# Windowed attention with keys at their position modulo 128, a V tile mixed by DMA, and proportions scaled by GpSimd

## The reference, cut to what matters

```python
def local_attention(q, k, v):                 # WINDOW = 64, QK_SCALE = 8
    bq = q.reshape(b, h, w, WINDOW, d) * QK_SCALE
    bk, bv = (look_around(bk), look_around(bv))   # the window before and this one
    sim = jnp.einsum('bhwid,bhwjd->bhwij', bq, bk)
    mask = (i < j) | (i > j + WINDOW) | (j == -1)
    attn = jax.nn.softmax(jnp.where(mask, -max, sim), axis=-1)
    out = jnp.einsum('bhwij,bhwjd->bhwid', attn, bv)

def _layer(x, ...):                           # 8 heads of 64 features
    q, k, v = split(shift_token(x) @ wqkv, 3)
    q, k = rotary_xpos(l2norm(q) * qs, l2norm(k) * ksc)
    x = x + local_attention(q, k, v) @ wo
    h = layernorm(shift_token(x)) * lg + lb
    a, g = split(h @ w1 + b1, 2)
    return x + (a * gelu(g)) @ w2 + b2
```

## Time and profile before

| what | value |
|---|---|
| median of 3 runs | 3171.33 us (3165.91 to 3173.92) |
| the profiled execution's own time | 3165.32 us |
| its span, first to last instruction | 3163.5 us |
| busy share of PE, DVE, ACT, POOL | 79%, 78%, 63%, 38% |
| first and last `reciprocals` of the first stack | 407.9 and 1354.0 us |
| the same of the second stack | 2176.7 and 3131.7 us |

### The profile page before, as it was taken

The page is one execution under the profiler, slowest core; times in us unless marked ns, Lnnn a source line. Parts: engine busy times, 40 slices in busy tenths (PEclk is TensorE's granted clock), DMA queues, the critical chain, the costliest instruction groups (busy, mean ns, idle before and its releaser), DMA issues. The chain is left out here.

```text
span 3163.5 us, 44621 instructions
## 1 busy us (share of the span) xinstructions
PE 2507.0 (79%) x12492; PEld 1338.3 (42%) x12492; DVE 2454.7 (78%) x5574; ACT 1977.9 (63%) x4833; POOL 1207.6 (38%) x1052
## 2 busy tenths in 40 slices
PE   7999688888888888866767667667888888888887
PEld 3555345445444444422222222223444545444444
DVE  2333388888888888848988989987888888888886
ACT  3444266666656665658777776765666666665664
POOL 1222232233332322228777777763333232223220
PEclk9999799999999999978888898898999999999999
DMA  2000000000000000000000000000000000000000
GB/s 116 1 0 0 1 1 1 1 1 1 1 1 1 1 0 0 1 0 1 1 1 1 0 1 0 0 1 1 1 1 1 0 1 1 1 8 4 4 4 11
DMA packets 1942, 13.50 MB, mean 4 GB/s; under 512 B 192, under 2 KB 192, under 8 KB 1216
## 3 DMA queue, kind: packets, MB, share of 16 engines
q1 hardware_dynamic: 1728, 11.24, 0.9%
HBM read 9.14 MB, written 2.10 MB: 4 GB/s over the span
## 5 line engine op out<-in xcount | busy, mean ns | idle before, releaser
L488 POOL TENSOR_TENSOR arena<-arena 128x512 f32<-128x512 f32 x256 | 325.1, 1270 | 1179.9 <-DVE arena L1439 1179.9
L1368 DVE RECIPROCAL RC<-LS 128x256 f32<-128x256 f32 x256 | 446.9, 1746 | 1.7 <-ACT P L1048 1.5
L514 POOL TENSOR_TENSOR arena<-arena 128x512 f32<-128x512 f32 x256 | 329.0, 1302 | 121.1 <-ACT arena L1208 117.8
L1076 ACT ACTIVATE arena<-psum 128x512 f32<-128x512 f32 x256 | 152.7, 596 | 313.0 <-PE psum L789 312.7
L492 POOL TENSOR_TENSOR arena<-arena,SC 128x512 f32<-128x512 f32 x256 | 267.3, 1044 | 197.6 <-DVE SC L1450 196.9
L1054 ACT ACTIVATE arena<-psum 128x512 f32<-128x512 f32 x256 | 152.6, 596 | 282.4 <-PE psum L699 270.2
L789 PE MATMUL psum<-rest,HA 128*128 128x512 f32 x512 | 277.3, 624 | 55.0 <-DVE arena L1439 55.0
L1525 DVE TENSOR_TENSOR_SCAN arena<-arena,psum 128x512 f32<-128x512 f32 x256 | 310.9, 1214 | 3.2
L740 PE MATMUL psum<-HN,rest 128*128 128x512 f32 (+1 forms) x384 | 217.8, 676 | 113.2 <-ACT arena L1091 79.5
L875 PE MATMUL psum<-BS,tabs 96*128 96x512 bf16 x384 | 143.4, 434 | 202.8 <-DVE arena L1525 201.2
L944 PE MATMUL psum<-arena,first 128*128 128x512 f32 x512 | 284.5, 644 | 11.6 <-POOL arena L505 11.2
(11 more groups left out here) (220 smaller groups left out, 6024.5 us busy)
## 6 DMA issues: line engine op xcount, KB each, us to landing
rest<-in_rest SPq DMA_DIRECT2D x1, 4183.0 KB, 22.5
X<-in_x SPq DMA_DIRECT2D x1, 2048.0 KB, 10.5
out<-X SPq DMA_DIRECT2D x8, 256.0 KB, 2.0
first<-in_first SPq DMA_DIRECT2D x1, 1445.5 KB, 6.1
tabs<-in_tabs SPq DMA_DIRECT2D x1, 1248.0 KB, 13.1
```

The source lines that it names most:

```text
L488: nc.gpsimd.tensor_tensor(CQ[:, part, :], CQ[:, part, :], SQN[:, part, :], ALU.add).then_inc(f_rope, 1)
L514: nc.gpsimd.tensor_tensor(WU[:, k % DEEP, :], RG[:, k % DEEP, :], U[t.j % 2][:, k % 2, :], ALU.mult).then_inc(m_wu, 1)
L1368: v.reciprocal(RC[:, 2 * (g % 2):2 * (g % 2) + 2, :].rearrange("p t (r d) -> p t r d", r=2), LS[:, g % 2, :, :].unsqueeze(3).to_broadcast( ...
```

## The change

1. Scores: every head has 2 x 128 columns of keys instead of 128 + 192. For the second 128 queries the key of position p stands in column p modulo 128: columns 128 to 191 of the bank hold keys 128 to 191 for all of these queries; columns 192 to 255 hold keys 64 to 127 for queries 128 to 191 and keys 192 to 255 for queries 192 to 255 (two products of 64 x 64 on halves of the output partitions). `band` follows this.
2. `maxima` and `exponentials`: four pieces of 128 x 128 per unit.
3. V: a mixed tile, whose lower 64 rows are keys 192 to 255 and whose upper 64 rows are keys 64 to 127, as `mixed_values` in the diff has it, is made per sequence by two DMAs of 64 x 512 fp32 from SBUF to SBUF, issued by SP. The output DMAs now stand in the same queue behind them, slot by slot.
4. `reciprocals` is 128 x 4 (`RS`). GpSimd multiplies the 128 x 512 proportions in `P` in place (`proportions`), between its two older operations.
5. `flip`: four transposes into one bank; the two banks alternate with the unit. ACT alone copies it (`flipped`), 128 x 512. `flipped_dve` is gone.
6. `weigh`: per head one product of 128 columns and two of 64. `output` is a plain copy. The wait for the output of the unit before moves from the copies to `weigh`.
7. Orders: on DVE `sums` and `products` come before `output`, and `reciprocals` before the third quarter step. On ACT both exponentials come first, `features` before `norms`, and the first two copies of V at the start of steps 1 and 2.

```diff
...
-BF, N_BF = layout([("ident16", 128), ("band", 384), ("causal", 384), ("sel", 32 * 128)])
+BF, N_BF = layout([("ident16", 128), ("band", 256), ("causal", 384), ("sel", 32 * 128)])
...
-        ARENA = 25088
+        ARENA = 27136
...
-        VT = [shared("layers", [128, 4, INNER]) for _ in range(2)]
+        VT = [shared("layers", [128, 6, INNER]) for _ in range(2)]
...
-        RC = sb("RC", [128, 4, 128])
-        P = sb("P", [128, 4, 384])
+        RS = sb("RS", [128, 2, 2, 2])
+        P = sb("P", [128, 4, 256])
...
-        f_rc = sem("f_rc")
+        f_rs = sem("f_rs")
+        f_rp = sem("f_rp")
-        f_ptd = sem("f_ptd")
...
+        f_vm = (sem("f_vm0"), sem("f_vm1"))
...
-    with sp_.Fori(0, PAIRS) as i:
-        sp_.wait_ge(f_x, i + (PAIRS + 1))
-        sp_.dma_start(out[:, bass.ds(i * NT, NT)], X[:, bass.ds(i * NT, NT)]).then_inc(out_done, 16)
+    def mixed_values(k, b):
+        v = VT[k.side(1)]
+        k.wait_ge(f_v, 4, 2 * b + 2, slot=1)
+        sp_.dma_start(v[0:64, 4 + b, :], v[0:64, 2 * b + 1, :]).then_inc(f_vm[b], 16)
+        sp_.dma_start(v[64:128, 4 + b, :], v[64:128, 2 * b, :]).then_inc(f_vm[b], 16)
+    def sp_slot(k):
+        if k.pre:
+            mixed_values(k, 0)
+            mixed_values(k, 1)
+        if k.ph and k.post and k.layer(-1) == DEPTH - 1:
+            k.wait_pair(f_x, -1)
+            sp_.dma_start(out[:, k.tokens(-1)], X[:, k.tokens(-1)]).then_inc(out_done, 16)
+    for ph in range(2):
+        passes(sp_, ph, sp_slot)
...
+    def rotated(k, m, n):
+        k.wait_ge(f_prod, 8, n + 1, slot=m)
+        nc.gpsimd.tensor_tensor(CQ[:, n % 2, :], CQ[:, n % 2, :], SQN[:, n % 2, :], ALU.add).then_inc(f_rope, 1)
+    def scaled(k, m, n):
+        k.wait_ge(f_rope, 8, n + 1, slot=m)
+        k.wait_ge(f_sc, 8, n + 1, slot=m)
+        heads = CQ[:, n % 2, :].rearrange("p (h d) -> p h d", d=DH)
+        nc.gpsimd.tensor_tensor(heads, heads, SC[:, n % 2, :].unsqueeze(2).to_broadcast([128, HEADS, DH]),
+                                ALU.mult).then_inc(f_qk, 1)
+    def proportions(k, m, g):
+        s = g % 2
+        k.wait_ge(f_rs, 8, g + 1, slot=m)
+        p = P[:, 2 * s:2 * s + 2, :].rearrange("p r (t c) -> p (r t) c", t=2)
+        nc.gpsimd.tensor_tensor(p, p, RS[:, s, :, :].rearrange("p r t -> p (r t)").unsqueeze(2).to_broadcast([128, 4, 128]),
+                                ALU.mult).then_inc(f_rp, 1)
     def pool_slot(k):
...
+        for g in range(8):
+            if item(k, 4 * g, 2):
+                rotated(k, *item(k, 4 * g, 2))
+            if k.heads(g + 1):
+                proportions(k, *k.heads(g + 1))
+            if item(k, 4 * g, 2):
+                scaled(k, *item(k, 4 * g, 2))
...
+        at = SEQ * b
...
+            mm(s[:, 0:128], q[rows, at:at + 128], key[rows, at:at + 128], start=True, stop=True)
...
+            mm(s[:, 128:192], q[rows, at + 128:at + 256], key[rows, at + 128:at + 192], start=True, stop=True)
+        for s, rows in halves:
+            mm(s[0:64, 192:256], q[rows, at + 128:at + 192], key[rows, at + 64:at + 128], start=True, stop=True)
+        for s, rows in halves:
+            mm(s[64:128, 192:256], q[rows, at + 192:at + 256], key[rows, at + 192:at + 256],
     def flip(k, m, g):
...
+        k.wait_ge(f_rp, 8, g + 1, slot=m)
+        k.wait_ge(f_pta, 8, g - 1, slot=m)
...
+            for tile in range(2):
+                at = 256 * r + 128 * tile
+                last = nc.tensor.transpose(P_BANK[g % 2][:, at:at + 128],
+                                           P[:, 2 * (g % 2) + r, 128 * tile:128 * tile + 128], F("ident"))
+        last.then_inc(f_ptp, 1)
     def weigh(k, m, g):
+        k.wait_ge(f_oe, 8, g, slot=m)
...
+            k.wait_ge(f_vm[b], 32, 32, slot=m)
+        v = VT[k.side(m)]
+        halves = [(O_BANK[64 * r:64 * r + 64, :], slice(DH * (2 * j + r), DH * (2 * j + r) + DH),
+                   PT[:, g % 2, 256 * r:256 * r + 256]) for r in range(2)]
+        for o, head, pt in halves:
+            mm(o[:, 0:128], v[:, 2 * b, head], pt[:, 0:128], start=True, stop=True)
+        for o, head, pt in halves:
+            mm(o[:, 128:192], v[:, 4 + b, head], pt[:, 128:192], start=True, stop=True)
+        for o, head, pt in halves:
+            last = mm(o[:, 192:256], v[:, 2 * b + 1, head], pt[:, 192:256], start=True, stop=True)
...
     def exponentials(k, m, g, r):
...
+        A(p[:, 0:128], p[:, 0:128], ACT.Exp, bias=NB[:, s, r, 0:1], scale=-1.0, accum_out=LS[:, s, r, 0:1])
+        A(p[:, 128:256], p[:, 128:256], ACT.Exp, bias=NB[:, s, r, 1:2], scale=-1.0,
+          accum_out=LS[:, s, r, 1:2]).then_inc(f_exp, 1)
+    def flipped(k, m, g):
+        k.wait_ge(f_pv, 8, g - 1, slot=m)
+        k.wait_ge(f_ptp, 8, g + 1, slot=m)
+        A(PT[:, g % 2, :], P_BANK[g % 2], ACT.Copy).then_inc(f_pta, 1)
...
+        if item(k, h, 7):
+            features(k, *item(k, h, 7))
...
+        if k.pre and h in (14, 30):
+            values(k, (14, 30).index(h) + 2)
     def act_slot(k):
         for g in range(8):
+            if k.pre and g in (1, 2):
+                values(k, g - 1)
             if k.heads(g + 1):
                 exponentials(k, *k.heads(g + 1), 0)
+                exponentials(k, *k.heads(g + 1), 1)
             if k.heads(g):
-                flipped_act(k, *k.heads(g))
-            act_dense(k, 4 * g)
-            if k.heads(g + 1):
-                exponentials(k, *k.heads(g + 1), 1)
-            for h in range(4 * g + 1, 4 * g + 4):
+                flipped(k, *k.heads(g))
+            for h in range(4 * g, 4 * g + 4):
                 act_dense(k, h)
...
     def maxima(k, m, g, r):
...
+        v.tensor_tensor_reduce(p[:, 0:128], S_BANK[r][:, 0:128], T16("band", 0, 128), -1.0, 3e38,
+                               ALU.add, ALU.min, NB[:, s, r, 0:1])
+        v.tensor_tensor_reduce(p[:, 128:256], S_BANK[r][:, 128:256], T16("band", 128, 256), -1.0, 3e38,
+                               ALU.add, ALU.min, NB[:, s, r, 1:2]).then_inc(f_nb, 1)
     def reciprocals(k, m, g):
...
+        v.reciprocal(RS[:, g % 2, :, :], LS[:, g % 2, :, :]).then_inc(f_rs, 1)
+    def before_maxima(k, g):
+        if k.heads(g):
+            k.wait_ge(f_ptp, 8, k.heads(g)[1] + 1, slot=k.heads(g)[0])
...
+            k.wait_ge(f_sim, 16, 2 * k.heads(g + 2)[1] + 2, slot=k.heads(g + 2)[0])
     def output(k, m, g):
...
+        k.wait_ge(f_pv, 8, g + 1, slot=m)
+        before_maxima(k, 8 * m + g + 1)
+        v.tensor_copy(OT[k.side(m)][:, j, SEQ * b:SEQ * b + SEQ], O_BANK[:, 0:256]).then_inc(f_oe, 1)
...
     def dve_slot(k):
         for g in range(8):
+            dve_dense(k, 4 * g)
             if k.heads(g - 1):
                 output(k, *k.heads(g - 1))
-            dve_dense(k, 4 * g)
-            if k.heads(g):
-                flipped_dve(k, *k.heads(g))
+            else:
+                before_maxima(k, g)
             if k.heads(g + 2):
                 maxima(k, *k.heads(g + 2), 0)
             dve_dense(k, 4 * g + 1)
             if k.heads(g + 2):
                 maxima(k, *k.heads(g + 2), 1)
-            dve_dense(k, 4 * g + 2)
             if k.heads(g + 1):
                 reciprocals(k, *k.heads(g + 1))
+            dve_dense(k, 4 * g + 2)
             dve_dense(k, 4 * g + 3)
...
+    k1 = np.where((q < 64) & (k >= 64), k, k + 128)
...
+    band = np.concatenate([ok0, ok1], 1)
```

61 lines of the change are left out of this document (removed).

## The result

The changed kernel takes 2901.68 us (median of 4 runs, 2894.18 to 2904.42), beside 3169.84 us of the kernel before on the same chip: ratio 0.915, 95% interval 0.9129 to 0.9172, 268 us less. The forecast was 2936 us, 235 less. The time is right within 35 us; of the reasons, half fell in the experiments, so part of the agreement is luck; the part on the prediction tells where.

The account below looks back on a forecast made before the run. DVE and PE, waiting for each other, were taken as the bound. Slots falling from 61.7 to 54.5 us gave 201 us over 28 slots, edges 34; 3165.3 less 235 is 2930, plus 6 is 2936 us, range 2860 to 3065.

Parts of the forecast that it names:

- What bounds the kernel: Both stacks: DVE and PE mostly run side by side but each waits for the other; 61.7 us per slot.
- Rival 1: PE, ACT and `T_BANK` hold steps 1 to 5; only steps 0, 6 and 7 shrink: 3059 us, chance 0.15.
- PE's block: `weigh`, `scores` and `flip` on PE: 2.01 us, at most 2.56, taken as 2.15, a gain of 0.34.
- the straight line: PE's score products: cost extrapolated from 192 and 128 columns, four of 64 at 0.21 us; block 2.01 us.
- rival 4: PE's small products cost their upper bound, 0.4 us more per step where PE ends last: 2996 us, within the forecast's 0.69.
- steps 4 and 5: Gelus keep 5.66 us, exponentials to `features` shrinks from 2.65 to 2.0, shorter block before: 16.5 us instead of 17.66.
- Steps 1 to 3: Three blocks give 1.0 us, 0.7 us DVE waits go in two steps, step 3 stays ACT's: 20.5 instead of 23.65.
- Step 0: `HA` written ahead of `sums` makes the `QK_BANK` cycle about 1 us longer: 5.4 us instead of 7.4.
- Step 6: Only PE's block shortens it: 6.2 us instead of 6.45.
- step 7: `to_features`, its copy, a V projection and `project` in a row: 5.4 us instead of 6.5.
- the cover: PE's other work between two flips just covers the 3.25 us from one flip through `output`, `reciprocals` and `proportions` to the next.
- Rival 3: DVE and GpSimd exclude each other, a slot needing 64.5 us: slower, 3250 us, chance 0.04.

Follow-up runs that it names:

- b1: The kernel before with only the reciprocal taken of 128 x 4 and a DVE copy spreading it to 128 x 256: 3166.98 us, ratio 0.9977.

## Why the prediction was right in the time and half wrong in the reasons

- **What bounds the kernel.** This step failed. The prediction took the 180.1 us before `output` for half of an exchange ("has PE waiting for DVE's copies on its other side"), and let DVE's relief shorten the steps. b1 shows that alone it does not, and PE's waits of the kernel before, shown there, could have told it: 1.7 us for DVE's flip copy and 11.2 for the reciprocals. Idle time before `output` shows that DVE waited for PE; that PE waited for DVE in turn was assumed. Rival 1 had the right premise (PE, ACT and `T_BANK` hold the steps) and the wrong time, since the change moved ACT's order as well.
- **DVE.** The groups' busy times drop by 607.6 us, as forecast (446.9 + 174.4 + 105.2 + 179.3 + 146.2 less 147.0 + 145.6 + 107.2 + 44.6). The engine's total is at 1983, not 1850: 85 us are on L1480, L1431, L1388 and L1389, some 15 are other small growth and 36 that groups overlap less.
- **PE's block.** 1.96 us, just under the straight line (2.01) and below the 2.15 taken; the bound of 2.56 for products of 64 x 64, and with it rival 4, is out. `scores` takes 0.87 us (607.51 to 608.38) for 0.95. 0.53 us less per unit at the rate of the doubled flip (63 us per 0.47) is 71 us, an estimate.
- **ACT.** The prediction gave its orders a place in steps 4 and 5 alone (16.5 us forecast, 16.50 measured) and none elsewhere. They are the largest part of the account below: 96 us for `exponentials` and `features`, 58 for the V copies. Of the 96, 15 are the clock of step 5, which the prediction did not have at all.
- **The sum from the runs.** 96 + 58 + 71 + 13 (the small reciprocal beside ACT's order, from two runs whose intervals overlap) = 238 of 268 us. This is an account and not a proof: 96 and 13 were measured in the kernel before, 58 and the rate of the 71 in the changed one. The remaining 30 can be DVE's order, its flip copy and the parts' influence on each other; no run assigns them. The parts aren't independent: ACT's order alone rids the kernel before of all its long steps 5, and the changed kernel has 9 of them again; and undone one at a time, five of them cost 165 + 134 + 63 + 58 + 37 = 457 us, the 37 with the tiny copies in it.
- **The steps.** Steps 1 to 3 were forecast at 20.5 and came to 18.76, since the V copies weren't seen. Step 0 was forecast at 5.4 and came to 6.66 from 7.05; `HA` before `sums` holds it more than the 1 us that was put down: its two writes take 831 + 587 ns and DVE idles 1.3 us before them (42.4 over 32). Step 6 5.93 for 6.2, step 7 5.34 for 5.4. Step 7's number was right with the wrong cause: the block gives 0.5 of its 1.5 us, ACT's order the rest. Steps 4 and 5 came out at 16.50 for 16.5, but with 0.5 us of clock in them that the forecast had not counted: the slot that it read (17.66 us) was a short one, the mean of the kernel before is 18.24. So the time of 2936 us owes something to luck: step 0 was 1.3 us too short in the forecast, steps 1 to 3 were 1.7 too long, and the two all but cancel.
- **Waits that were added.** PE idles 1.1 us in all behind `proportions` and 11.0 behind the scaling: the cover that the prediction named holds. `output` waits 42.4 us. The mixing DMAs land in 2.3 us each, and no wait of PE is put down to them; to leave them out wasn't tried.
- **Rival 3** (DVE and GpSimd exclude each other throughout) is out as a time. In the small it is there: the prediction named "if DVE's operations grow while POOL runs" as a sign of being wrong, and four lines of them did (L1480, L1388, L1389, L1431). It confined such growth to the shifts and the layer norms' products and left out L1480, which grew most (49.9 us). See below.

## What to carry to other kernels

Idle time of an engine that is busy four fifths shows who it waits for, not that its own length counts: ask what ends the waits of the engine on its other side, and here that was ACT's place for one copy. Where one bank has many users, put the copy that empties it first in its queue, and fill the time before it with work that is ready. A relief that gives nothing in the kernel before can be worth 165 us in the changed one, so test it in both; and look where the work stands when it is put back, since here it also came to stand ahead of a new chain over GpSimd. A step that has two lengths from slot to slot is a reason to look at the granted clock early.
